# Row stacks of the first sequence built by matmuls, and a new order of steps, in a gated cross-attention and mixture-of-experts block

## The reference, cut to what matters

```python
x = x + tanh(g_xattn) * cross_attention(layernorm(x), ctx)        # one head of 128
h = rmsnorm(layernorm(x)) ; q, k, v = h@wq, h@wk, h@wv            # 16 heads of 8
X = layernorm(x) + softmax(q k^T * 8**-0.5) v @ wo
h2 = rmsnorm(X)
probs = softmax(h2 @ router_w); top 2 of 8 experts, their weights through a softmax
shared = swiglu(h2, sh_gate, sh_up, sh_down)                      # FF = 256
spec = sum over experts of combine_e * swiglu(h2, e_gate, e_up, e_down)
out = x + tanh(g_ffn) * (X + shared + spec)
```

## Time and profile before

| | us |
|---|---|
| median of 3 runs | 245.76 (245.37 to 247.09) |
| the profiled execution, its own time | 245.03 |
| its span in the trace | 243.2 |
| PE busy | 198.6 (82%) |
| DVE busy | 155.4 (64%) |
| ACT busy | 100.4 (41%) |
| POOL busy | 46.1 (19%) |

### The profile page before, as it was taken

How to read it: one execution, slowest core, us unless ns; L and a number is a source line. 1 busy time by engine, 2 the same in 40 slices (tenths; PEclk the granted TensorE clock), 3 DMA queues, 4 the chain that set the end, 5 groups by cost and what they waited for, 6 DMA issues and landing times.

```text
span 243.2 us, 4326 instructions
## 1 busy us (share of the span) xinstructions
PE 198.6 (82%) x1543; PEld 172.0 (71%) x1543; DVE 155.4 (64%) x402; ACT 100.4 (41%) x199; POOL 46.1 (19%) x71
## 2 busy tenths in 40 slices
PE   7793875087582999889888589999999699999995
PEld 5461753075471876767767478887999699999994
DVE  2868363158758566576677865646778875565553
ACT  2753223000441578777578355562232322212220
POOL 3776011014004026312842000110011000000000
PEclk9999595559889599999999999999999979999999
DMA  5939435555305873577400000000000000000000
GB/s 153 280 83 170 71 56 64 64 64 64 37 24 67 98 114 89 66 95 125 131 1 1 3 0 0 3 0 4 0 24 0 0 3 22 4 0 26 0 0 24
DMA packets 10102, 12.34 MB, mean 51 GB/s; under 512 B 1088, under 2 KB 8128, under 8 KB 9888
## 3 DMA queue, kind: packets, MB, share of 16 engines
q1 hardware_dynamic: 10080, 12.05, 29.2%
HBM read 5.50 MB, written 0.52 MB: 25 GB/s over the span
## 4 chain that ended last, share of the span: by engine, by line
PE 55%; DVE 22%; issue 6%; DMA 5%; SPq 4%; ACT 4%; POOL 3%; DVEq 0%; POOLq 0%; ACTq 0%
PE bank L1034 11%; PE bank L1023 6%; PE bank L1022 6%; PE bank L1024 5%; PE bank L1005 5%; PE bank L979 5%; PE bank L990 5%; SPq L301 4%; DMA k_st<-split 4%; DVE mxs L781 4%; PE bank L888 3%; DVE y L657 3%; DVE early L791 2%; PE bank L905 2%; DVE early L798 1%
## 5 line engine op out<-in xcount | busy, mean ns | idle before, releaser
L781 DVE TENSOR_REDUCE mxs<-bank 128x2 f32<-128x512 f32 x64 | 42.0, 687 | 18.5 <-PE bank L979 18.1
L557 ACT ACTIVATE ep<-bank 128x512 f32<-128x512 f32 x64 | 37.0, 601 | 24.3 <-PE bank L990 23.7
L1022 PE MATMUL bank<-split,whi 128*128 128x256 f32 x144 | 43.4, 301 | 0.0
L1034 PE MATMUL bank<-down_s,early 128*128 128x128 f32 x288 | 39.2, 280 | 2.6 <-DVE early L798 2.5
L1023 PE MATMUL bank<-split,whi 128*128 128x256 f32 x144 | 40.8, 284 | 0.0
L1024 PE MATMUL bank<-split,wlo 128*128 128x256 f32 x144 | 40.5, 281 | 0.0
L979 PE MATMUL bank<-k_st,q_st 80*128 80x256 f32 x128 | 32.3, 337 | 9.2 <-DMA k_st<-split 7.8
L1034 PEld LDWEIGHTS bank<-down_s,early 128*128 128x128 f32 x288 | 35.8, 195 | 3.4 <-DVE early L798 2.9
L979 PEld LDWEIGHTS bank<-k_st,q_st 80*128 80x128 f32 x128 | 21.5, 207 | 16.0 <-issue 13.5
L1022 PEld LDWEIGHTS bank<-split,whi 128*128 128x128 f32 x144 | 27.6, 192 | 0.0
L1023 PEld LDWEIGHTS bank<-split,whi 128*128 128x128 f32 x144 | 27.5, 191 | 0.0
(11 more groups left out here) (135 smaller groups left out, 287.9 us busy)
## 6 DMA issues: line engine op xcount, KB each, us to landing
raw<-expert_w SPq DMA_DIRECT2D x9, 256.0 KB, 8.1
q_st<-split SPq DMA_DIRECT2D x32, 64.0 KB
k_st<-split SPq DMA_DIRECT2D x32, 64.0 KB
k_st<-k_st SPq DMA_DIRECT2D x6, 256.0 KB, 5.5
down_s<-expert_w SPq DMA_DIRECT2D x9, 128.0 KB, 8.0
early<-ctx_T SPq DMA_DIRECT2D x1, 672.0 KB, 8.0
xs<-x_tiles SPq DMA_DIRECT2D x2, 256.0 KB, 4.4
out_dram<-x SPq DMA_DIRECT2D x4, 128.0 KB, 1.8
```

Source lines behind the costliest of these rows:

```text
L557: nc.scalar.activation(ep[:, n % NEP].rearrange("p t s -> p (t s)"), b_of(("exp", n))[:], ACT.Exp, scale=SCALE_H).then_inc(free(("exp", n) ...
L781: nc.vector.tensor_reduce(mxs[:, half % 2, :, 64 + h:65 + h], b_of(("max", n))[:].rearrange("p (t s) -> p t s", t=TB), AX_X, ALU.max).then ...
L1022: pe.matmul(bank, whi[:, fs], h2hi[:, hs], start=True, stop=False)
L1034: last = pe.matmul(b_of(("down", n))[:, j * D:(j + 1) * D], act_t[:, n % 2, f * L + j * P:f * L + (j + 1) * P], down_s[:, f, e * D:(e + 1) ...
```

## The change

Stack 0 is no longer built by DMAs. POOL builds two sets of selection matrices in `select_rows` (step `j0`), in the place that experts 6 and 7 take later. In four steps `e0` to `e3` PE multiplies the split rows of sequence 0 by them, 8 matmuls of 256 columns in each step; ACT copies the key rows out in two instructions of 32x512, DVE the query rows in one of 64x512. Each step gives the stacks of four heads, and slots 0, 4, 8, 12 wait for one step each. SP's list loses `stack(sp, 0, ...)`; `split` of sequence 2 waits for the last selection matmul instead of the DMAs.

The lists are arranged anew. In the start the padding is cleared later, and `h1`, `k1`, `w0` and `s5` move behind the first slots. The tail steps get their own offsets in each sequence, with distances between filling and reading. Items: one after slot 58, two after 70, one after 74 and 75, then 95, 101, 125, 126, two after 129, 133: 12 in all; the slots reach to 136, and 24 items follow.

```diff
 NSTACK = 3
-M_STEPS = [("mT0", 8, 8), ("mT1", 16, 16)]
-C_STEPS = [("uT0", 30, 30), ("uT1", 31, 31), ("cT", 33, 33), ("wo", 35, 35), ("square", 36, 36), ("h2", 37, 37),
-           ("h2T", 40, 40), ("router", 42, 42)]
-ROUTE_STEPS = [("route_exp1", 42, 42), ("route_top", 44, 44), ("route_exp2", 44, 44), ("route_weights", 45, 45)]
-FIRST_STEPS = """f0 g0 xn0 f1 z0 q0 g1 s0 xn1 s1 p0 f2 q1 o0 p1 s2 g2 o1 s3 n0 p2 xn2 h0 o2 k0 p3 t0
-                 q2 o3 s4 n1 w0 f3 s5 h1 p4 k1""".split()
-MIXED_STEPS = {0: "g3 o4", 1: "p5 xn3", 2: "o5", 3: "q3 n2", 4: "s6", 5: "s7", 6: "h2", 7: "p6 w1", 8: "k2 o6 m0", 9: "p7",
-               10: "o7", 11: "n3 m1", 13: "h3", 15: "k3 m2 m3", 18: "m4", 27: "c3", 31: "w2", 42: "m5 m6 m7 m8", 47: "w3"}
+SEQ_STEPS = {
+    0: [("mT0", 9, 9), ("mT1", 17, 17), ("uT0", 30, 31), ("uT1", 31, 31), ("cT", 32, 32),
+        ("wo", 38, 41), ("square", 38, 41), ("h2", 38, 44), ("h2T", 45, 45), ("router", 54, 56)],
+    1: [("mT0", 7, 7), ("mT1", 16, 17), ("uT0", 31, 31), ("uT1", 31, 31), ("cT", 31, 31),
+        ("wo", 34, 35), ("square", 39, 39), ("h2", 40, 42), ("h2T", 43, 45), ("router", 47, 50),
+        ("route_exp1", 46, 50), ("route_top", 48, 52), ("route_exp2", 51, 55),
+        ("route_weights", 49, 58)],
+    2: [("mT0", 8, 8), ("mT1", 15, 15), ("uT0", 31, 34), ("uT1", 34, 35), ("cT", 35, 35),
+        ("wo", 40, 41), ("square", 40, 45), ("h2", 44, 49), ("h2T", 54, 60), ("router", 58, 61)],
+    3: [("mT0", 8, 9), ("mT1", 16, 16), ("uT0", 36, 36), ("uT1", 37, 44), ("cT", 41, 46),
+        ("wo", 50, 52), ("square", 50, 55), ("h2", 52, 55), ("h2T", 58, 58), ("router", 59, 60),
+        ("route_exp1", 69, 72), ("route_top", 64, 75), ("route_exp2", 70, 76),
+        ("route_weights", 88, 88)],
+}
+FIRST_STEPS = """f0 g0 xn0 q0 f1 s0 g1 f2 xn1 z0 s1 p0 g2 q1 xn2 p1 o0 o1 s2 s3 t0 n0 q2 p2 j0 f3 p3 s4 h0 o2 o3
+                 k0 g3 p4 e0 n1 xn3""".split()
+MIXED_STEPS = {1: "h1 s5 m0", 2: "k1", 3: "e1 p5 q3", 4: "o4 e2 o5 m1 e3", 6: "w0", 7: "s6 s7 p6 n2 h2", 11: "k2",
+               12: "p7 o6", 13: "w1 o7", 15: "n3", 16: "m2", 21: "h3", 23: "m3", 27: "k3 m4", 31: "c3", 40: "w2",
+               42: "m5 m6 m7", 56: "w3", 58: "i0", 70: "i0 i0", 74: "i0", 75: "i0", 76: "m8", 95: "i0", 101: "i0",
+               125: "i0", 126: "i0", 129: "i0 i0", 133: "i0"}
...
+        sel_q, sel_k = (w[:, (NEXP - 3) * 2 * FF:(NEXP - 1) * 2 * FF].rearrange("p (c g m) -> p c g m", c=2, g=NG)
+                        for w in (whi, wlo))
...
             for b in range(1, NSTACK):
                 copy_pads(sp, b)
-            stack(sp, 0, (0, 1))
             for b in range(1, NSTACK):
                 stack(sp, b, (0, 1))
...
+            def select_rows():
+
+                step(nc.gpsimd.memset(sel_q.rearrange("p c g m -> p (c g m)").bitcast(F32), 0.0))
+                step(nc.gpsimd.memset(sel_k.rearrange("p c g m -> p (c g m)").bitcast(F32), 0.0))
+                heads = ident[:].rearrange("p (i d g) -> p i g d", i=2, d=DH)
+                for part in range(2):
+                    for i in range(2):
+                        one = heads[:, i].unsqueeze(2).broadcast_to([P, NG, 2, DH])
+                        rows_q = sel_q[:, part, :, 32 * i:32 * i + 32].rearrange("p g (a c d) -> p g a c d", a=2, c=2)
+                        nc.gpsimd.tensor_copy(rows_q[:, :, part], one).then_inc(sel_ready, 1)
+                        rows_k = sel_k[:, part, :, 32 * i:32 * i + 32].rearrange("p g (a c d) -> p g a c d", a=2, c=2)
+                        nc.gpsimd.tensor_copy(rows_k[:, :, :, part], one).then_inc(sel_ready, 1)
...
+                if e == NEXP - 3:
+                    is_full(pool, ("stk", NQ - 1))
...
                 elif stage == "z":
-                    pool.wait_ge(norm1_out, 2)
-                    pool.wait_ge(xb_ready, 1)
+                    pool.wait_ge(norm1_out, 3)
+                    pool.wait_ge(xb_ready, 2)
                     clear_pads(i)
...
                 if b >= 2:
-                    act.wait_ge(stacked[b - 2], 256)
+                    if b == 2:
+                        is_full(act, ("stk", NQ - 1))
+                    else:
+                        act.wait_ge(stacked[b - 2], 256)
...
+            def stack_keys(i):
+                gs = 2 * i
+                if i == 0:
+                    act.wait_ge(pads_ready, 1)
+                is_full(act, ("stk", i))
+                nc.scalar.copy(k_st[0:32, 0, gs:gs + 2, :].rearrange("p g s -> p (g s)"),
+                               b_of(("stk", i))[0:32]).then_inc(k_half, 1)
+                nc.scalar.copy(k_st[32:64, 0, NG + gs:NG + gs + 2, :].rearrange("p g s -> p (g s)"),
+                               b_of(("stk", i))[32:64]).then_inc(free(("stk", i)), 1)
...
+            def stack_queries(i):
+                is_full(dve, ("stq", i))
+                nc.vector.tensor_copy(q_st[0:64, 0, 2 * i:2 * i + 2, :].rearrange("p g s -> p (g s)"),
+                                      b_of(("stq", i))[0:64]).then_inc(free(("stq", i)), 1)
...
+            def make_stacks(i):
+                if i == 0:
+                    pe.wait_ge(sel_ready, 8)
+                    pe.wait_ge(hi_ready, 1)
+                    written(("qk2", 0))
+                for qk, use, rows in ((0, ("stq", i), sel_q), (1, ("stk", i), sel_k)):
+                    may_fill(pe, use)
+                    for n in range(2):
+                        for part in range(2):
+                            last = pe.matmul(b_of(use)[0:64, n * L:(n + 1) * L], rows[:, part, 2 * i + n, :],
+                                             split[:, 0, part, qk, :], start=(part == 0), stop=(part == 1))
+                    last.then_inc(full(use), 1)
...
-                        pe.wait_ge(stacked[b], 256)
+                        if b > 0:
+                            pe.wait_ge(stacked[b], 256)
+                    if n % 4 == 0 and b == 0:
+                        written(("stq", n // 4))
+                        written(("stk", n // 4))
```

More of the change, by code:

```diff
@@ L88, in flamingo_block @@
     for b in range(NB):
-        steps = M_STEPS + C_STEPS + (ROUTE_STEPS if b % 2 else [])
-        for step, fill, read in steps:
+        for step, fill, read in SEQ_STEPS[b]:
             fill_at.setdefault(16 * b + fill, []).append((step, b))
@@ L97, in flamingo_block @@
     dense += [(e, b) for b in range(2, NB) for e in range(NEXP)]
+    dense = [dense[n] for n in ITEMS] if ITEMS else dense
     ND = len(dense)
-    last_exp = SLOTS_A
     order = [step_of(text) for text in FIRST_STEPS]
@@ L110, in flamingo_block @@
         order.append(("a", i))
-        order += [step_of(text) for text in MIXED_STEPS.get(i, "").split()]
-        if i in EARLY_AT or i >= EARLY_FROM and (i - EARLY_FROM) % EARLY_EVERY == 0:
+        for text in MIXED_STEPS.get(i, "").split():
+            if text[0] != "i":
+                order.append(step_of(text))
+                continue
             order += item(begun)
-            if i <= last_exp:
-                tanh_items.append(begun)
+            tanh_items.append(begun)
             begun += 1
@@ L137, in flamingo_block @@
             uses.append(("proj", ("qk2", i)))
+        if stage == "e":
+            uses += [("misc", ("stq", i)), ("misc", ("stk", i))]
         if stage == "w":
@@ L362, in norm1 @@
                 nc.gpsimd.tensor_tensor(small[:, 8, ts], small[:, 0, ts], neg_half[:, 0], ALU.pow).then_inc(norm1_out, 1)
+                pool.wait_ge(norm1_out, b + 1)
             def norm2(b):
@@ L367, in norm2 @@
                 nc.gpsimd.tensor_tensor(small[:, 5:7, ts], small[:, 3:5, ts], neg_half[:], ALU.pow).then_inc(norm2_out, 1)
+                pool.wait_ge(norm2_out, b + 1)
             def norm3(b):
@@ L373, in norm3 @@
                 nc.gpsimd.tensor_tensor(small[:, 11, ts], small[:, 7, ts], neg_half[:, 0], ALU.pow).then_inc(norm3_out, 1)
+                pool.wait_ge(norm3_out, b + 1)
             def clear_pads(s):
@@ L394, in add_bias @@
                                         ALU.add).then_inc(xb_ready, 1)
+                pool.wait_ge(xb_ready, b + 1)
             def split_weights(e):
@@ L403, in split_weights @@
                 nc.gpsimd.tensor_tensor(wlo[:, ws], words, whi[:, ws].bitcast(F32), ALU.subtract).then_inc(w_split, 1)
+                pool.wait_ge(w_split, e + 1)
             def split_h2(b):
@@ L413, in split_h2 @@
                                         ALU.subtract).then_inc(h2s_ready, 1)
+                pool.wait_ge(h2s_ready, b + 1)
             def tables():
@@ L420, in tables @@
                 nc.gpsimd.tensor_copy(router_pad[:, 0:NE], router_s).then_inc(router_ready, 1)
+                pool.wait_ge(router_ready, 1)
             for stage, i in order:
@@ L438, in _ @@
                     tables()
+                elif stage == "j":
+                    select_rows()
                 elif stage == "m":
@@ L588, in _ @@
                     h_turned(i)
+                elif stage == "e":
+                    stack_keys(i)
```

(4 more changed lines are left out.)

5 lines of the change are left out of this document (2 added, 3 removed).

## The result

The changed kernel takes 228.44 us in the median (227.42 to 230.42, 4 executions), and the kernel before took 246.29 on the same chip (245.37 to 247.09). The ratio is 0.930, interval 0.926 to 0.934. The forecast was 231.8, range 223.0 to 240.0.

A forecast was written before the change was run, and what follows sets the result against it. The prediction took items to bound the kernel from 143.5 us, with no engine full before and the first sequence's DMA stack costing 19.2 us. Its terms -14.9 + 1.0 - 5.3 + 5.3 = -13.9 gave 231.8 against 245.76, range 223 to 240.

The forecast's parts named there:

- likeliest case: Whole kernel: the forecast's own case, a time of 228 to 236.5 us, chance 0.58.
- first head: Start up to slot 0: slot 0 begins at about 35 us instead of 49.84, -14.9 us.
- slots 0 to 15: First 16 slots: added steps +2.6 us, less DVE idle time; +1.0 taken, bounds -2 and +4.
- slots 16 to 63: Middle slots: waits -3, one item moved out -2.3, low clock -1, stack 3 +1; -5.3 us, bounds -9 and +2.
- the rest: From slot 64 on: one more item after the slots +2.3 us, more stalls; +5.3 taken, bounds +1 and +12.
- The stack by matmuls: Start, first sequence's stack: matmuls and copies take 3.1 us instead of 19.2, 16.1 gained, with 1.0 lost before the split ends.
- steps that stand further apart: Slots 0 to 15: wider spacing should take some of the 7 us in which DVE is idle there.
- slower rival: Last tail stands bare: PE idles 11 us, its clock falls to 0.50, 3 us more; 255 us in all, chance 0.06.
- stack 3: Slot 48 waits for this DMA stack, landing 18.9 us after slot 27; 1 us added for the chance of it.
- the rival of the stack DMAs: Slots 32 and 48 wait some 3 us each beyond the forecast for DMA stacks; 238 us, chance 0.13.
- a low clock in the last tail: Tail of the last sequence: named as a sign that the prediction would be wrong.
- The larger gain: Tail stalls go nearly whole: slots 16 to 63 -9, last stage +1.5, slots 0 to 15 0; 223.4 us, chance 0.19.

The follow-up runs named there:

- e6: Changed kernel with four more memsets of 128x1024 on POOL ahead of the selection rows: 227.83 us, ratio 0.922.
- e1: Kernel before with stack 0 by selection matmuls, all else in the old lists: 242.09 us, ratio 0.984.
- e3: Changed kernel's new lists, but stack 0 by 16 DMAs as before, without j0 and e0 to e3: 243.3 us, ratio 0.979.
- e2: As e1, old start up to slot 42, but with the changed kernel's tail steps and items: 240.77 us, ratio 0.978.
- e4: Changed kernel with the old tail step distances in sequences 0 to 2 (fill and read in the same slot): 236.44 us, ratio 0.951.
- e7: Changed kernel with sequence 1's steps from square on, and the routing of sequences 0 and 1, at their old slots: 238.66 us, ratio 0.962.
- e9: Changed kernel with h0 ahead of s4, k0 ahead of o2 and o3, e0 ahead of o3 in the start: 229.64 us, ratio 0.935.
- e11: Changed kernel with POOL's first three weight splits waiting for DVE's second norms of sequences 1, 2, 3: 223.78 us, ratio 0.910.
- e13: Changed kernel with POOL's first three splits behind DVE's norms, 15 items in the last tail, twelve useless PE matmuls in the start: 219.78 us, ratio 0.893.
- e5: Changed kernel with 15 items instead of 12 in the tail of the last sequence: 225.37 us, ratio 0.917.

## Why the prediction was right

The forecast was 231.8 and the changed kernel took 228.4, 3.4 us less, at the lower end of the prediction's likeliest case. In the spans it is 13.9 us forecast and 16.2 measured, and the terms are: first head -14.9, measured -13.6; slots 0 to 15 +1.0, measured -2.8; slots 16 to 63 -5.3, measured -5.6; the rest +5.3, measured +5.8. So three of four hold, and one is mis-sized.

**The stack by matmuls: right.** Slot 0 was put at 35 us, -14.9; it starts at 35.73, -14.1, and the first maximum starts 13.6 earlier. The split of `k0` was to be done at 31.7 and was at 32.8. `e0` was priced at 1.7 us and took 1.14 (33.08 to 34.22), ACT's two copies at 1.2 in all and took 1.15. Selection rows were forecast at 28.5 and came at 29.16; the cover was put at 3 us and is 3.9, and e6 uses it up. What the sum left out is that DVE would be last. It priced a norm beside POOL for `n0` alone, though its text warned of any `n` step there; it is `n1` (1.96 us instead of 0.60) that the first maximum waits for.

**Slots 0 to 15: the term that was mis-sized.** Taken at +1.0 with bounds -2 and +4; measured -2.8, outside them. By PE's own slots it is more: slot 16 starts at 64.22 instead of 82.40, where the prediction had 67.8 instead of 81.6. Its positive part was right: +2.6 for the added steps, and e1 against before, after against e3, give +2.7 and +2.4. The part for steps that stand further apart was set at -1.6 and is -5.2 (e3 against before) to -5.3 (after against e2). Half of it, 2.7 us, is the same contention: in before the norms of sequences 2 and 3 took 1.97 and 1.95 us in L657, both beside a split of POOL (its subtraction ran from 59.49 and from 76.66), and after they take 0.60 each, at 54.22 and 66.72, where POOL is still. Both lie on the chain that ended last in before, so that their length counts there, at least until another chain takes over:

```profile
58.88 1.98 DVE y L657 x2
...
76.06 1.96 DVE y L657 x2
```

The subtraction beside the first of them, in POOL's timeline:

```profile
59.49 1.27 POOL L403 TENSOR_TENSOR wlo<-raw,whi 128x512 fp32r<-128x512 f32 x1
```

Where the other half lies stays open; no run tells the steps of the new order apart.

**Slots 16 to 63: right in sum, not in its parts.** -5.3 forecast, -5.6 measured; that the two are so near is luck. The stages are +1.5, -2.1 and -5.0. The -2.1 fits the item that moves out of slot 47, priced at -2.3. The -5.0 is the distances between filling and reading in sequence 1: they were counted at 3 us in all, e4 prices them at 5 to 8, and e7 shows that the steps from `square` to the routing weights of sequence 1 carry all of it, by waits of PE and by a clock that falls to 0.50 behind them. The prediction had this mechanism, but in its slower rival and for the last tail. The +1.5 in heads 17 to 33 was not foreseen: the clock there is 0.93, where the kernels with 1.00 (e9, e11, e13) take 16.5 or 16.6 us instead of 17.7. No wait for a stack shows in the waits of PE after, at any of slots 16, 32 and 48, so that the +1 for stack 3 was not needed, and the rival of the stack DMAs fell.

**From slot 64 on: right.** +5.3 forecast, +5.8 measured. PE idle of 4 to 8 us in the last tail was named as what would show it; it is 4.4. e5 gives the other proof: three items put there take 2.6 us back. One of the prediction's own signs of being wrong did show, a low clock in the last tail (0.57 over 152 to 156 us), but for a few microseconds and behind 1.8 us of waiting, not behind the 11 of its slower rival.

The larger gain (223.4, or 227 with half of it) had its chance of 0.19 for stalls of the tails that go nearly whole. e5, with 225.4, goes that way in the last tail. e11 and e13 reach 223.8 and 219.8 with a granted clock nearer 1.00 in the start, a gain that the prediction did not have.

## What to carry to other kernels

When a long wait is taken away, list what was hidden beneath it and move that in the same edit; each half of this change alone gave 1.6 and 2.1%, both gave 7%. Behind short waits of PE, look at the granted clock before the busy share: in e7 a wait of 2.3 us was followed by 12 us at half speed, and in e13 matmuls without use in three gaps of the start held the clock up. Before moving work earlier on one engine, look at which engine truly ends last there, what the moved steps now stand in front of, and which engine works beside it. And where a kernel's clock varies from one execution to the next, an edit is judged by all of them, not by the one that was profiled.
